# Attention results stored by the token's remainder modulo eight before the selecting matmuls

## The reference, cut to what matters

```python
_L1_attn_ref: q = (xn @ Wq + bq) -> (B, S, 8, 16); k likewise; v = xn @ Wv + bv, 1024 wide
softmax over all 512 keys, times v, one result of 16 values for each token and head
x = x + _L1_attn_ref(_layernorm(x, axis=-1), ...)
```

## Time and profile before

| what | value |
|---|---|
| time, median of 3 runs | 748.29 us (745.18 to 751.69) |
| the profiled execution's own time | 749.26 us |
| its span in the trace | 747.5 us |
| mean granted TensorE clock | 0.924 of full |
| PE / PEld busy | 627.8 us (84%) / 371.6 us (50%) |
| DVE / ACT / POOL busy | 528.3 us (71%) / 365.3 us (49%) / 315.2 us (42%) |
| softmax attention's steps with `probs` | about 488 to 617 us of the span |

### The profile page before, as it was taken

How to read it: one execution, slowest core, us unless ns; L and a number is a source line. 1 busy time by engine, 2 the same in 40 slices (tenths; PEclk the granted TensorE clock), 3 DMA queues, 4 the chain that set the end, 5 groups by cost and what they waited for, 6 DMA issues and landing times. The chain is left out here.

```text
span 747.5 us, 14245 instructions
## 1 busy us (share of the span) xinstructions
PE 627.8 (84%) x5189; PEld 371.6 (50%) x5189; DVE 528.3 (71%) x979; ACT 365.3 (49%) x598; POOL 315.2 (42%) x286
## 2 busy tenths in 40 slices
PE   3668788999999999999988776697888988679991
PEld 2245555667666676666756544221432355335440
DVE  5778769898887987978885567666566354636772
ACT  1323333675675757657566322265455662127760
POOL 2765536555545546465471333320000100546772
PEclk9878899999999999999999997679999997889996
DMA  7330010100101101101011502588131610012224
GB/s 250 79 106 30 16 30 9 29 16 22 31 9 30 22 16 30 23 16 24 16 30 57 127 2 67 109 184 199 57 114 56 255 59 0 26 57 56 72 62 131
DMA packets 31872, 47.15 MB, mean 63 GB/s; under 512 B 5520, under 2 KB 21948, under 8 KB 30524
## 3 DMA queue, kind: packets, MB, share of 16 engines
q1 hardware_dynamic: 30268, 43.09, 21.9%
q0 software_dynamic: 1536, 3.16, 1.3%
HBM read 29.12 MB, written 9.46 MB: 52 GB/s over the span
## 5 line engine op out<-in xcount | busy, mean ns | idle before, releaser
L612 POOL TENSOR_TENSOR rnorm<-ssum_c,neg_half 128x16 f32<-128x16 f32 x32 | 94.3, 2946 | 109.7 <-DVE ssum_c L1014 108.0
L1174 DVE TENSOR_REDUCE mneg<-ps 128x2 f32<-128x1024 f32 x64 | 76.3, 1219 | 38.7 <-PE ps L1619 38.5
L624 POOL TENSOR_TENSOR region_r<-region_b,region_d 128x512 f32<-128x512 f32 x64 | 82.8, 1315 | 39.9 <-DVE region_b L1019 39.4
L842 ACT ACTIVATE region_r<-ps 128x1024 f32<-128x1024 f32 x64 | 64.4, 1024 | 45.0 <-PE ps L1632 44.9
L590 POOL TENSOR_TENSOR var_eps<-mv,eps 128x4 f32<-128x4 f32 x20 | 7.0, 349 | 154.6 <-DVE mv L956 154.6
L744 ACT ACTIVATE region_a<-ps 128x1024 f32<-128x1024 f32 x32 | 32.8, 1025 | 64.8 <-PE ps L1404 64.8
L1403 PE MATMUL ps<-region_d,hT 128*128 128x512 f32 x64 | 38.8, 691 | 20.1 <-DVE region_b L1019 19.3
L729 ACT ACT_TABLE_LOAD x39 | 50.0, 1283 | 1.4 <-PEq L1868 0.7
L1019 DVE TENSOR_TENSOR region_b<-ps,rnorm 128x1024 f32<-128x1024 f32 x32 | 39.1, 1222 | 11.6 <-POOL rnorm L612 10.8
L1489 PEld LDWEIGHTS ps<-region_d,oT 128*128 128x128 f32 x256 | 36.2, 206 | 19.6 <-issue 12.9
L1517 PE MATMUL ps<-region_a,region_d 128*114 128x512 f32 x96 | 45.6, 598 | 0.3 <-ACT region_a L761 0.3
(11 more groups left out here) (225 smaller groups left out, 1427.7 us busy)
## 6 DMA issues: line engine op xcount, KB each, us to landing
region_a<-in_wgu SPq DMA_DIRECT2D x16, 512.0 KB, 3.6
region_b<-region_a SPq DMA_DIRECT2D x56, 130.0 KB, 2.3
region_d<-in_wd SPq DMA_DIRECT2D x4, 1024.0 KB, 5.9
parts_dram<-region_b SPq DMA_DIRECT2D x6, 384.0 KB, 2.7
xs_dram<-region_a SPq DMA_DIRECT2D x1, 2064.0 KB, 7.9
pts<-xs_dram SPq DMA_DIRECT2D x32, 64.5 KB, 1.8
region_d<-in_wqkv SPq DMA_DIRECT2D x2, 768.0 KB, 9.3
region_b<-parts_dram SPq DMA_DIRECT2D x4, 384.0 KB, 6.0
```

The costliest lines, as they stand in the source:

```text
L612: g.tensor_tensor(rnorm[:, :], ssum_c[n % 2][:, :], neg_half[:, :], ALU.pow).then_inc(S["rnormed"], 1)
L624: g.tensor_tensor(dst, src, tab, ALU.mult).then_inc(S["rot_bb"], 1)
L842: act_(dst, bank(l1_bank[what, b, i], of=2), ACT.Exp).then_inc(T["ex"], 1)
L1174: d.tensor_reduce(mneg[b % 2][:, 2 * i:2 * i + 2], bank(l1_bank[what, b, i], of=2) .rearrange("p (q t) -> p q t", q=2), AX.X, ALU.max, neg ...
```

## The change

ACT's copy reads the bank in order, as before, and writes token 8 r + l to column 64 l + r: for consecutive tokens the write address steps by 64 elements. PE reads the 64 columns of remainder l from 64 neighbouring columns, where it took every eighth before. Number, size and order of the instructions, all waits, the moving operand and the output addresses in PSUM stay.

```diff
@@ ACT, steps ("probs", 10) and "end"
-                    act_(at_sb[hg], bank(6 + hg), ACT.Copy).then_inc(T["at_sb"], 1)
+                    act_(at_sb[hg].rearrange("p (l r) -> p r l", l=GRP), bank(6 + hg).rearrange("p (r l) -> p r l", l=GRP),
+                         ACT.Copy).then_inc(T["at_sb"], 1)
@@ PE, step "end"
-                        cols = at_sb[hg].rearrange("p (r l) -> p r l", l=GRP)
+                        cols = at_sb[hg].rearrange("p (l r) -> p l r", l=GRP)
...
-                                last = mm(dst, cols[:, :, l], sel[:, par, :].rearrange("p (j g) -> p j g", j=2),
+                                last = mm(dst, cols[:, l, :], sel[:, par, :].rearrange("p (j g) -> p j g", j=2),
```

## The result

The changed kernel is faster: 735.71 us (median of 6 runs, 734.45 to 740.37) against 747.98 (6 runs); the ratio is 0.9859, 95% interval 0.9821 to 0.9898, which is 10.5 us less (7.6 to 13.4); the two medians alone lie 12.3 us apart. The forecast was 742.6, 5.7 us less, and its range began at 737.5. The sign was right; the forecast gain is little more than half of what came.

The account below looks back on a forecast made before the run. PE's strided loads were taken to bound the four selecting-matmul stretches, 16.25 us together. Loads 7.8 us less, minus 1.13 and 0.93 for copies, gave 5.7 us less: 742.6 from the median of 748.29, range 737.5 to 747.5.

Parts of the forecast that it names:

- Loads: PE's four selecting-matmul stretches: 29 ns a pair instead of 60, each 2.12 us instead of 4.06, 7.8 us less.
- the bounds of 25 and 31 ns: Range for the pace of a load with its matmul in the four stretches: 8.9 and 7.2 us less.
- Bank 7 copies: ACT's copies within the four ends: covered at the first two, PE stalls 0.65 and 0.28 us after, 0.93 together.
- Bank 6 copies: ACT's copies ahead of the exponentials, 0.43 us longer each: 0.22 + 0.22 + 0.26 + 0.43 charged, together 1.13 us.
- Sum of the work: Gain of the loads less the charges for both banks' copies: 7.8 - 1.13 - 0.93 = 5.7 us less.
- Clock: Rival: TensorE's half clock after second and fourth end goes (2.7 us, 739.9) or another comes (744.4); chance 0.17.
- the 1.8 us that I priced behind the fourth end: Time lost at L1556 after the fourth end, where four matmul records took 3.67 us at half clock.
- Copies free: Rival: ACT's strided writes aren't slowed, only 0.23 us of stall is left, 7.6 us less, 740.7; chance 0.26.
- Loads not it: Rival: PSUM writes or matmul issue set PE's 60 ns, stretches stay 4.06 us, 748.3 to 749.4; chance 0.10.
- Slower: Rival: ACT's write pays by the step's size, a copy takes 5.6 us, time 777 us; chance 0.05.

Follow-up runs that it names:

- strided twice: The kernel before the change with every selecting matmul issued twice, still loading every eighth column: 767.54 us, ratio 1.0211.

## Why the prediction fell short

*Loads: right.* 29 ns a pair and 2.12 us a stretch were forecast, 2.06 came where nothing stalls. (For the bounds of 25 and 31 ns the same working gives 8.8 and 7.3 us less, not 8.9 and 7.2; nothing hangs on it.) The row at L1470 was the right neighbour, and the rival that PSUM's writes or issue set the pace is out.

*Bank 7 copies: right.* 1.02 us forecast, 1.06 measured; covered at the first two ends, stalls of 0.65 and 0.28 us forecast at the others, 0.68 and 0.32 measured (2.79 and 2.43 us to the reciprocal against 2.11). The four stretches with their reciprocals' release were 16.4 us and are 9.4: 7.0 less, where the prediction had 7.8 - 0.93 = 6.9.

*Bank 6 copies: too dear.* 1.13 us were charged, 0.4 is what the gap between third and fourth end shows (22.6 to 23.0). The first three cost nothing. ACT's timeline in the changed kernel:

```profile
505.10 1.06 ACT L848 ACTIVATE oT<-ps 128x512 f32<-128x512 f32 x1
505.93 1.08 ACT L842 ACTIVATE region_r<-ps 128x1024 f32<-128x1024 f32 x1
507.86 1.02 ACT L842 ACTIVATE region_r<-ps 128x1024 f32<-128x1024 f32 x1 [0.86 <-PE ps L1633]
```

The exponentials behind the copy began 0.83 us after the copy's start, while it still ran, where they had begun 0.80 us after it (508.66 and 509.46). The next ones came 2.76 us after the copy's start and had come after 2.77. The fourth copy, with no gap behind it, cost what was charged for it.

*Sum of the work:* 7.0 - 0.4 = 6.6 us against the 5.7 forecast. That alone would have given 741.7, inside the range.

*Clock: the step that failed.* The sum took the clock as unchanged, a term of nothing, and put its fall into a rival with a chance of 0.17, at 2.7 us, read from one trace. In the three traces of the kernel before, the gap behind the second end averages 24.46 us and is 22.20 in the changed kernel: 2.3 us. The one between third and fourth averages 25.74 against the 22.6 that the copy leaves it: 3.1 us. Together 5.4, which with 6.6 makes the 12.0 us between the mean ways through the ends (95.6 and 83.6). The measured 10.5 (7.6 to 13.4) is compatible with that; by whole runs the part beyond the work is 10.5 - 6.6 = 3.9 us (1.0 to 6.8). The 2.3 us behind the second end are shown to come from the slow loads. The 3.1 us rest on two of three traces of the kernel before against none of three of the changed one, and what brings that fall is open.

The trace I argued from was the mildest of three: it had not the late fall between third and fourth end. It did have half clock right behind the third end (589.3 to 592.5, the row shown above), which the prediction's reading left out and which cost nothing. And the 1.8 us that I priced behind the fourth end come and go: L1556 took 3.67 us for its four records in the first trace of the kernel before, 1.98 in the second and 3.32 in the third, and 1.98 or 1.99 in all three of the changed kernel, so about 1.0 us on average. Behind the fourth reciprocal the spans run on for 129.3 us on average before and 128.5 after. The second and the third trace:

```profile
617.92 1.98 PE L1556 MATMUL ps<-region_b,region_r 128*128 128x512 f32 x4
```

```profile
616.53 3.32 PE L1556 MATMUL ps<-region_b,region_r 128*128 128x512 f32 x4
```

The 3.4 us ahead of the first end were chance: over three traces each the first selecting matmul came at 521.5 and 521.6 us on average.

*Order of the rivals.* Copies free: no for writes. Loads not it: no. Slower: no. Clock: yes, together with the forecast rather than instead of it, and that is why a range built on one at a time missed.

## What to carry to other kernels

If a short series of small fp32 matmuls bounds a stage, compare its load duration with the nearest line that loads as many neighbouring columns; here 217 against 138 ns told 7 us. Put the stride on the PSUM side of the copy in front of it, where it was free, and keep steps of 16 bytes or more off the SBUF side. Before pricing a stage from one trace, ask whether the clock fell in it: stages of slow loads can drag the clock of the next one down, and a second and third trace of the same kernel show how much. Price a fall by the gap that it lengthens: the one right behind the third end lengthened none.

## What the runs showed of the hardware

- A step of 8 bytes between fp32 elements in SBUF is free for ACT's writes (0.62 us) and PE's loads, one of 16 bytes costs the full price: 1.09 us, and loads at 60 ns a pair in place of 29. The Trainium skill, "SBUF — State Buffer" (Door 1: The DMA port swizzle), puts the free range of fp32 at four elements; here four elements already cost all, and two were free. The same passage asks for two accesses to a 16-byte line, and that fits both: a step of 8 bytes makes two, one of 16 bytes one.
- ACT reads PSUM at a step of 8 elements (32 bytes) at full pace: 594 ns for 128 x 512. PE writes PSUM in two runs of 17 columns at 29 ns a pair, where one run of 65 went at 31.
- ACT begins an instruction 0.23 us before a strided copy ahead of it ends (505.93 against 506.16), and 0.11 us before an in-order one ends (kernel before, 605.74 against 605.85).
- Loads at a step of 8 elements go at the same pace at either clock: in "strided twice" the first stretch, all at 1.2 GHz, and the others, which began at 2.4, each took 7.90 us.
- TensorE was granted 1.2 GHz behind the second stretch of slow loads in 7 of 7 traces and in none of the 10 traces of other kernels at the same place.
